# A two-block sequence model in one launch: counting the ties of the 32nd score, and loading the expert stage's weights one stage earlier

## The chip, the cores and the metric

The kernel runs on one core of a Trainium2 chip. Its time is the device time of one execution in microseconds (us); of several executions the median is given. The engines are named as in the profile: PE (TensorE matmul; PEld is its weight load), DVE (VectorE), ACT (ScalarE), POOL (GpSimd) and SP (SyncE, which here only issues transfers). All arrays are float32 unless said otherwise.

## What is computed

Four sequences of 256 tokens and 256 channels, with a context of 4096 tokens and 192 channels each, go through six residual stages in turn:

```
x = x + cross_attention(layernorm(x), ctx, ...)          # 16 heads over 4096 context tokens
x = x + linear_attention(layernorm(x), ...)              # second order, decaying, 16 heads
x = x + experts(layernorm(x), ...)                       # 8 experts, top 1, low-rank parts
x = x + topk_cross_attention(layernorm(x), ctx, ...)     # below; then a state space layer and an FFN
x = x + causal_attention(layernorm(x), ...)
x = x + fp4_linear(layernorm(x), ...)
```

The change touches the third and the fourth. The fourth keeps, for each query row and each of 4 heads, the 32 largest of the 4096 scores:

```
scores = einsum('bthd,bghd->bhtg', Q, K) / sqrt(32)
scores = where(vision_mask, scores, -inf)
topv, topi = top_k(scores, 32)
probs = softmax(topv)
attn = zeros_like(scores).at[..., topi].set(probs)
c_t = einsum('btg,bgd->btd', attn.mean(heads), V)
```

## The kernel before, in words

Everything is one program with a hand-written order for each engine. It is built of stages (`stage_x0`, `stage_hla`, `stage_moe`, `stage_x1a`, `stage_x1b`, `stage_a1`); each returns one function per engine, and each engine runs them one after the other. Between two stages stands a barrier (`stage_end`): each of the four compute engines signals its end, and every engine, SP too, waits for all the others.

**The linear attention** (`stage_hla`, about 880 to 1092 us of the span) takes its weights from `OV`, which were loaded during the first stage; its function for SP is empty (`pass`).

**The expert stage** (`stage_moe`, about 1092 to 1251 us) weaves four jobs: the experts of the 4 sequences, the convolution kernel of the later state space layer ("s4d"), and the keys of the first sequence for the next stage ("keys"). SP starts it with three loads (L1404 to L1406): `x1a` (256 KB, the projections for keys and queries), `moe` (2756 KB) and `s4d` (645.5 KB), and then the context blocks `CT` of `key_projection`, two buffers of 96 KB that are refilled as PE uses them (L1067). DVE starts with the layernorm of sequences 0 and 1 (`XN`, L204), then does the s4d setup (L1292 on), which needs `z_dt`, an exponential by ACT (L1212) from the `s4d` pack. PE starts with the first two pieces of the keys, then transposes `XN`, does two more pieces and then the gate products (`LG`).

**The selection stage** (`stage_x1a`, about 1251 to 1834 us) goes through 16 pieces p (4 sequences by 2 blocks of 128 query rows by 2 pairs of heads), two heads h in each. In outline:

- PE computes the scores of a piece in 8 parts; ACT copies them into `SC[p % 2]`, after the selection of piece p - 2 has freed it.
- DVE takes the 8 largest of each group of 128 scores (`candidates`, L1674), 32 groups, so 256 candidates in `CA` (128x256). `top(p, h)` (L1676 to L1690) then finds the 32nd value: four rounds of `match_replace` (which removes the 8 values found) and `max` (the next 8). The fourth round is there for the 33rd value alone.
- A flag per row says where the short way can't be trusted: when the 33rd value equals the 32nd, or when a group of 128 may hold more than 8 of the 32 (its 8th candidate is at least the 32nd value). PE adds up the flags of all rows (`flag`), and `check(p)` reads the sum into a register; if it isn't 0, a slow way over all 4096 scores is taken.
- ACT computes the exponentials of the piece into `PM` (`weigh`, L1604). DVE then keeps those at or above the 32nd value and sums them (`select`, L1716, a `scalar_tensor_tensor` over 4096 with its sum written out).
- POOL divides by the sums and adds the four heads up in `ACC` (L1787 to L1797): for even p a scaling (head 0), and a scaling and an addition (head 1); for odd p a scaling and an addition for both.

DVE's order in this stage: in step n it does the candidates and `top` of piece n - 1, and `check` and `select` of piece n - 2, behind the first head's candidates where n is even and in their middle where n is odd. Where n % 4 is 3 it also converts a mask row (`MR`, L1667), and where n % 4 is 1 it normalises the next queries (`XN`, L1660), both ahead of the candidates.

```
for r8 in range(4):
    if r8 > 0:
        e.wait_ge(*V.now())
    e.match_replace(CA[:, :], t8[:, 8 * r8:8 * r8 + 8], CA[:, :], SENT).then_inc(*V.up())
    e.wait_ge(*V.now())
    e.max(t8[:, 8 * r8 + 8:8 * r8 + 16], CA[:, :]).then_inc(*V.up())
```

## Time and profile before

| | |
|---|---|
| median of 3 runs | 2200.42 us (2195.33 to 2202.61) |
| the profiled execution | 2203.82 us, of which its span 2202.0 us |
| busy over the span | PE 82%, DVE 56%, ACT 47%, POOL 35% |
| DVE, 8 largest of 128 scores (L1674) | 1024 times, 275 to 277 ns |
| DVE, `top`: match_replace and max over 256 | 128 of each, 409 and 428 ns |
| DVE, `select` (L1716) | 32 times, 4484 ns |
| POOL, addition into `ACC` (L1797) | 22 times, 8872 ns |
| POOL, scalings (L1795, L1792) | 30 times, 3.68 us |
| POOL, reciprocal of a sum (L1787) | 30 times, 0.55 to 4.73 us |

The times of the profile are those of one execution. "Idle before" is how long the engine stood before an instruction, with what ended that wait. An engine that isn't the bottleneck may idle at no cost, so the busy shares over the whole span say little here: each stage has its own limit.

### The profile page before, as it was taken

To read this page: it belongs to the slowest core of one execution; us is meant where nothing else is said; L and a number is where in the kernel's file an instruction comes from. 1 tells how busy PE (TensorE), PEld (TensorE's weight loads), DVE (VectorE), ACT (ScalarE), POOL (GpSimd) and SP (SyncE) were. 2 spreads that over 40 slices of the span, in tenths; PEclk is the share of its full clock that TensorE was granted. 3 is DMA by queue.
4 is the path that set the end of the run, shared out by engine and by line. 5 is a ranking of instruction groups with operands and counts; after the bars stand their busy time and mean duration, and the time that the engine had idled before them with its cause. 6 is when DMAs were issued, how large, how long until landed. Compare 5 with 4: busy or idle time off the path is not lost. (4 is left out here: it accounts for less than half of the span.)

```text
span 2202.0 us, 34851 instructions
## 1 busy us (share of the span) xinstructions
PE 1807.5 (82%) x13676; PEld 1104.1 (50%) x13676; DVE 1233.7 (56%) x3075; ACT 1025.5 (47%) x1381; POOL 759.8 (35%) x669
## 2 busy tenths in 40 slices
PE   5969999999999898888687877877766849888874
PEld 2434554454445444556466723544444437676653
DVE  5142424333332300364578379899999995557675
ACT  1457657756765687112131145555546521214442
POOL 6343324433542230000030027777878850110000
PEclk8989999999999999999967855878787669999897
DMA  6647555655756170000120001223132252000000
GB/s 143 118 105 127 117 109 109 117 119 113 122 109 128 56 125 38 1 2 1 58 70 1 14 1 44 79 59 87 51 86 66 58 184 86 1 1 1 1 6 15
DMA packets 78046, 150.01 MB, mean 68 GB/s; under 512 B 15464, under 2 KB 63144, under 8 KB 71464
## 3 DMA queue, kind: packets, MB, share of 16 engines
q1 hardware_dynamic: 64304, 101.80, 16.5%
q0 software_dynamic: 12768, 42.59, 12.7%
q8 instruction: 118, 1.93, 0.4%
q10 hardware_dynamic: 792, 3.17, 0.4%
q14 instruction: 64, 0.52, 0.1%
HBM read 93.59 MB, written 2.62 MB: 44 GB/s over the span
## 5 line engine op out<-in xcount | busy, mean ns | idle before, releaser
L571 ACT ACTIVATE P<-R 128x1024 f32<-128x1024 f32 x512 | 506.8, 1026 | 222.3 <-PE R L112 186.3
L112 PE MATMUL R<-QS,KST 100*128 100x256 bf16 x2048 | 297.0, 277 | 60.2 <-ACT P L571 53.5
L112 PEld LDWEIGHTS R<-QS,KST 100*128 100x128 bf16 x2048 | 170.0, 98 | 224.8 <-ACT P L571 120.9
L1797 POOL TENSOR_TENSOR ACC<-ACC,PM 128x4096 f32<-128x4096 f32 x22 | 195.2, 8872 | 1.8
L200 POOL TENSOR_TENSOR LNrs<-LNve,pk_const 128x2 f32<-128x2 f32 x36 | 25.3, 703 | 462.7 <-DVE LNve L196 462.5
L112 PE MATMUL R<-OV,QT 32*128 32x512 f32 x512 | 183.0, 802 | 0.0
L789 POOL DMA_DIRECT2D KST<-OV x300 | 144.5, 490 | 71.7 <-PE R L112 55.2
L112 PE MATMUL R<-P,VP 128*32 128x256 f32 x2304 | 156.1, 388 | 5.3 <-issue 5.0
L601 DVE CAST OV<-RT 128x512 bf16<-128x512 f32 x64 | 27.7, 432 | 217.2 <-ACT RT L116 130.0
L733 POOL CAST OV<-RT 128x512 bf16<-128x512 f32 x64 | 42.6, 665 | 266.5 <-DVE RT L604 266.5
L1787 POOL TENSOR_TENSOR SM<-SM,NG 128x1 f32<-128x1 f32 x30 | 79.3, 2644 | 147.5 <-DVE PM L1716 147.5
L112 PE MATMUL B<-P,VP 128*32 128x256 f32 x1792 | 121.2, 388 | 0.0
L1674 DVE MAX8 CA<-S 128x8 f32<-128x128 f32 x512 | 101.8, 275 | 12.0 <-ACT S L116 11.6
L1674 DVE MAX8 CA<-SC 128x8 f32<-128x128 f32 x512 | 100.9, 277 | 4.8 <-ACT SC L116 4.1
L116 ACT ACTIVATE S<-R 128x1024 f32<-128x1024 f32 x64 | 64.1, 1023 | 60.1 <-DVE PM L1716 34.3
L112 PEld LDWEIGHTS R<-P,VP 128*32 128x32 f32 x2304 | 60.7, 109 | 61.9 <-issue 36.2
L112 PE MATMUL R<-OV,ONB 1*128 1x512 bf16 x256 | 62.9, 488 | 33.9 <-ACT SC L116 20.8
L112 PEld LDWEIGHTS R<-OV,QT 32*128 32x128 f32 x512 | 65.1, 251 | 38.7 <-issue 30.9
L112 PE MATMUL R<-CN,AT 128*128 128x192 f32 x288 | 67.0, 385 | 19.1 <-DMA CN<-in_ctxn 13.6
L116 ACT ACTIVATE SC<-R 128x1024 f32<-128x1024 f32 x64 | 64.1, 1020 | 39.6 <-PE R L112 24.3
L1795 POOL TENSOR_SCALAR PM<-PM,SM 128x4096 f32<-128x4096 f32 x22 | 80.9, 3679 | 2.2
L1716 DVE SCALAR_TENSOR_TENSOR PM<-SC,T,PM 128x4096 f32<-128x4096 f32 x16 | 71.1, 4484 | 9.8 <-ACT S L116 4.2
(370 smaller groups left out, 3559.0 us busy)
## 6 DMA issues: line engine op xcount, KB each, us to landing
KST<-OV POOLq DMA_DIRECT2D x276, 128.0 KB, 10.8
CT<-in_ctxP SPq DMA_DIRECT2D x40, 768.0 KB, 4.4
CN<-in_ctxn SPq DMA_DIRECT2D x60, 384.0 KB, 3.5
CT<-in_ctxT SPq DMA_DIRECT2D x64, 192.0 KB, 2.5
KST<-OV SPq DMA_DIRECT2D x84, 128.0 KB, 10.4
KST<-in_ctxP ACTq DMA_DIRECT2D x4, 768.0 KB, 9.4
QS<-x_q POOLq DMA_DIRECT2D x24, 128.0 KB, 5.4
pk_a<-in_pk_a SPq DMA_DIRECT2D x1, 3014.0 KB, 10.4
```

Of the source, the lines that this page charges most:

```text
L112: return e.matmul(o, l, r, start=st, stop=sp, skip_group_check=True)
L116: return e.activation(o, i, ACT.Copy)
L200: return e.tensor_tensor(LNrs[:, i, :], LNve[:, i, :], cst["nhalf"], ALU.pow)
L571: e.activation(P[(32 * p + k0) % 3][:, :], ring.at(("s", p, k0))[:, :], ACT.Exp).then_inc(*EX.up((p, k0)))
L601: e.tensor_copy(KS[0][:, cs], rt[:, :]).then_inc(*KD.up())
L733: e.tensor_copy(KS[1][:, cs], rt[:, :]).then_inc(*KG.up())
L789: e.dma_start(KST[buf][16 * s:16 * s + 16, hh, cols], KS[SLOT_K[s]][r0:r0 + 16, cols]).then_inc(*S[buf].up((b, g) if hh == hs[-1] and s == ...
L1674: e.max(CA[:, g * 8:g * 8 + 8], SC[p % 2][:, h, g * 128:g * 128 + 128]).then_inc(*V.up())
L1716: e.scalar_tensor_tensor(pm[:, :], SC[p % 2][:, h, :], T8[p % 2][:, h, 31:32], pm[:, :], ALU.is_ge, ALU.mult, accum_out=SM[p % 3][:, h, SU ...
L1787: e.tensor_tensor(rc, sm[:, h, SUM:SUM + 1], NG1[:, :], ALU.pow).then_inc(*G.up())
L1795: e.tensor_scalar(pm, pm, rc, 0.25, ALU.mult, ALU.mult).then_inc(*G.up())
L1797: e.tensor_tensor(acc[:, :], acc[:, :], pm, ALU.add).then_inc(*G.up(("sum", p, h)))
```

## The change

It has two parts that have nothing to do with each other.

1. **`top` and `check`.** The fourth round is dropped. In its place one `tensor_scalar` compares the 256 entries left in `CA` with the 32nd value and writes its sum out: the number of entries at or above it, which is 8 if there is no tie. The flag is then (8th candidate of a group at least the 32nd value) plus that number, so the sum over 128 rows and two heads is 2 * 128 * 8 when all is well, and `check` branches when it is anything else.

2. **The expert stage's first loads.** A new function `moe_loads` allocates the `moe` and `s4d` packs and the two `CT` buffers so that they live through both stages. SP issues the three loads and the first two `CT` blocks in the linear attention's stage, where it had nothing to do. The order among the three loads is now `s4d`, `x1a`, `moe`.

```
-        def stage_hla(c):
+        def stage_hla(c, loads):
...
             def sync(e):
-                pass
+                loads(e)
...
+        def moe_loads(c, x1a):
+            t = {nm: pack(c, nm) for nm in ("moe", "s4d")}
+            keys = key_projection(c, x1a[1])
+            LW, W4 = dsig("w_moe"), dsig("w_s4d")
+
+            def sync(e):
+                load(e, "s4d", t["s4d"][0], W4)
+                load(e, "x1a", x1a[0], LA)
+                load(e, "moe", t["moe"][0], LW)
+                keys["sync"](e, 0, 0)
...
             def sync(e):
-                load(e, "x1a", x1a[0], LA)
-                load(e, "moe", t_moe, LW)
-                load(e, "s4d", t_s4, W4)
                 for kind, *at in plan:
-                    if kind == "keys":
+                    if kind == "keys" and at[1] > 0:
                         keys["sync"](e, *at)
...
-                    for r8 in range(4):
+                    for r8 in range(3):
...
                     e.wait_ge(*V.now())
-                    e.tensor_scalar(fl, fl, t8[:, 32:33], t8[:, 31:32], ALU.max, ALU.is_ge).then_inc(*V.up(("fl", p, h)))
+                    e.tensor_scalar(CA[:, :], CA[:, :], t8[:, 31:32], 0.0, ALU.is_ge, ALU.add, accum_out=t8[:, 32:33]).then_inc(*V.up())
+                    e.wait_ge(*V.now())
+                    e.tensor_scalar(fl, fl, t8[:, 31:32], t8[:, 32:33], ALU.is_ge, ALU.add).then_inc(*V.up(("fl", p, h)))
...
-                    with e.If_ne(reg["v"], 0):
+                    with e.If_ne(reg["v"], 2 * 128 * 8):
...
-        with ExitStack() as c:
-            stages.append(stage_hla(c))
         KL = sbt(ctx, "KL", [128, 2, 256])
         x1a = pack(ctx, "x1a")
-        with ExitStack() as c:
-            stages.append(stage_moe(c, x1a))
+        with ExitStack() as both:
+            early = moe_loads(both, x1a)
+            with ExitStack() as c:
+                stages.append(stage_hla(c, early["sync"]))
+            with ExitStack() as c:
+                stages.append(stage_moe(c, early))
```

The other lines of the diff hand `bank` to `key_projection`'s functions when they are called, no longer when it is built.

On SP, around the barriers into the linear attention and out of it, the order before (OV<-in_pk_hla is the linear attention's own pack, issued in the first stage; CT_91 and CT_92 are the two context buffers):

```order
L222 DMA OV<-in_pk_hla 128x4864 [waits d_k_slots1,d_k_slots_pool1,d_k_slots_pool0,d_k_slots0]
L222 DMA pk_x1a<-in_pk_x1a 128x512 [waits stage_end_tensor,stage_end_vector,stage_end_gpsimd,stage_end_scalar]
L222 DMA pk_moe<-in_pk_moe 128x5512
L222 DMA pk_s4d<-in_pk_s4d 128x1291
L1067 DMA CT_91<-in_ctxT 96x2x256
L1067 DMA CT_92<-in_ctxT 96x2x256
L1067 DMA CT_91<-in_ctxT 96x2x256 [waits x1_key_product]
```

and in the changed kernel:

```order
L222 DMA OV<-in_pk_hla 128x4864 [waits d_k_slots1,d_k_slots_pool1,d_k_slots_pool0,d_k_slots0]
L222 DMA pk_s4d<-in_pk_s4d 128x1291 [waits stage_end_scalar,stage_end_gpsimd,stage_end_vector,stage_end_tensor]
L222 DMA pk_x1a<-in_pk_x1a 128x512
L222 DMA pk_moe<-in_pk_moe 128x5512
L1082 DMA CT_52<-in_ctxT 96x2x256
L1082 DMA CT_53<-in_ctxT 96x2x256
L1082 DMA CT_52<-in_ctxT 96x2x256 [waits stage_end_gpsimd,stage_end_scalar,x1_key_product,stage_end_vector,stage_end_tensor]
```

Before, the barrier at the end of the linear attention stood ahead of all five transfers; now it stands behind them, ahead of the third `CT` block, and they wait only for the barrier at the end of the first stage.

On DVE, one call of `top` in the selection stage before (CA holds the candidates, T the values found, SM the flag and the negated maximum):

```order
L1679 TENSOR_REDUCE SM_146<-CA 128x1
L1680 MAX T_144<-CA 128x8
L1682 TENSOR_SCALAR SM_146<-T_144 128x1
L1686 MATCH_REPLACE CA<-T_144,CA 128x256
L1688 MAX T_144<-CA 128x8
L1686 MATCH_REPLACE CA<-T_144,CA 128x256
L1688 MAX T_144<-CA 128x8
L1686 MATCH_REPLACE CA<-T_144,CA 128x256
L1688 MAX T_144<-CA 128x8
L1686 MATCH_REPLACE CA<-T_144,CA 128x256
L1688 MAX T_144<-CA 128x8
L1690 TENSOR_SCALAR SM_146<-SM_146,T_144 128x1
```

and the same call in the changed kernel:

```order
L1689 TENSOR_REDUCE SM_146<-CA 128x1
L1690 MAX T_144<-CA 128x8
L1692 TENSOR_SCALAR SM_146<-T_144 128x1
L1696 MATCH_REPLACE CA<-T_144,CA 128x256
L1698 MAX T_144<-CA 128x8
L1696 MATCH_REPLACE CA<-T_144,CA 128x256
L1698 MAX T_144<-CA 128x8
L1696 MATCH_REPLACE CA<-T_144,CA 128x256
L1698 MAX T_144<-CA 128x8
L1701 TENSOR_SCALAR CA,T_144<-CA,T_144 128x256
L1703 TENSOR_SCALAR SM_146<-SM_146,T_144 128x1
```

The fourth pair is gone and one pass over the 256 candidates with two outputs (L1701) stands in its place, so DVE has one instruction fewer in each of the 32 calls.

## Rows read from the trace of the kernel before

**Rows 1.** Busy time by stretch: start of the experts, its first 40 us, selection
```profile
core 0: us, PE busy (x) PEld busy (x) DVE busy (x) ACT busy (x) POOL busy (x), PEclk, DMA share, GB/s
1092.00:1105.00 13.00, 0.06 (x1) 0.09 (x1) 4.20 (x16) 0.42 (x1) 1.95 (x4) 0.63 0.83 318
1105.00:1145.00 40.00, 33.64 (x91) 24.13 (x92) 31.62 (x49) 15.85 (x24) 8.79 (x6) 0.54 0.23 70
...
1310.00:1834.00 524.00, 384.52 (x1696) 241.48 (x1697) 474.26 (x1500) 271.73 (x242) 383.35 (x82) 0.74 0.26 77
```

**Rows 2.** Timeline (start, duration, instruction, idle before), start of the expert stage
```profile
1092.50 0.33 SPq L222 DMA_DIRECT2D pk_x1a<-in_pk_x1a  x1
...
1097.21 0.73 DVE L204 TENSOR_SCALAR XN<-X,LNmv,LNrs 128x256 f32<-128x256 f32 x2 [0.81 <-POOL LNrs L200]
...
1104.23 0.42 ACT L1212 ACTIVATE z_dt<-pk_s4d 128x256 f32<-128x256 f32 x1 [16.57 <-DMA pk_s4d<-in_pk_s4d]
1104.75 0.42 DVE L1292 TENSOR_TENSOR z_pi<-z_dt,pk_s4d 128x256 f32<-128x256 f32 x1 [6.81 <-ACT z_dt L1212]
1104.94 3.75 PE L112 MATMUL B<-CT,pk_x1a 96*128 96x256 f32 x8 [13.45 <-DMA CT<-in_ctxT]
```

**Rows 3.** Timeline, expert stage, from the gate to the first expert product
```profile
1120.34 0.57 ACT L116 ACTIVATE OV<-B 128x512 f32<-128x512 f32 x1
...
1122.26 3.47 PE L112 MATMUL B<-pk_moe,XT 128*128 128x40 f32 x16
...
1124.13 0.24 DVE L1338 TENSOR_TENSOR LG<-B,pk_moe 128x80 f32<-128x80 f32 x1 [4.88 <-PE B L112]
...
1136.19 1.10 PE L178 MATMUL B<-pk_const,LM 128*32 128x128 f32 x4 [2.40 <-ACT OV L116]
...
1145.53 1.55 PE L112 MATMUL R<-XT,pk_moe 128*128 128x256 f32 x4
```

**Rows 4.** Timeline, DVE, the fourth round of one `top`
```profile
1486.65 0.09 DVE L1686 MATCH_VALUE_LOAD CA<-T,CA 128x8 f32 x1
...
1487.17 0.43 DVE L1688 MAX8 T<-CA 128x8 f32<-128x256 f32 x1
1487.63 0.27 DVE L1690 TENSOR_SCALAR SM<-SM,T 128x1 f32<-128x1 f32 x1
```

**Rows 5.** Prices near the added pass: durations of L1660 (min/median/max), a sum written out
```profile
L1660 DVE TENSOR_SCALAR XN<-X,MV,RSD x8: 401/410/1673, 1253.2 to 1532.9; 128x256 f32<-128x256 f32 x8
...
1578.77 0.08 DVE L1716 DVE_READ_ACCUMULATOR PM<-S,T,PM 128x1 f32 x1
```

**Rows 6.** Timeline, DVE and POOL: instructions of DVE held by POOL
```profile
1105.43 2.11 DVE L1294 TENSOR_TENSOR z_t<-pk_s4d 128x256 f32<-128x256 f32 x1
...
1523.90 8.91 POOL L1797 TENSOR_TENSOR ACC<-ACC,PM 128x4096 f32<-128x4096 f32 x1
...
1531.29 1.67 DVE L1660 TENSOR_SCALAR XN<-X,MV,RSD 128x256 f32<-128x256 f32 x1
```

**Rows 7.** Timeline, POOL's last addition of an odd piece and DVE's next `select`
```profile
1565.72 8.84 POOL L1797 TENSOR_TENSOR ACC<-ACC,PM 128x4096 f32<-128x4096 f32 x1
...
1574.36 4.48 DVE L1716 SCALAR_TENSOR_TENSOR PM<-S,T,PM 128x4096 f32<-128x4096 f32 x1 [0.60 <-DVE FI L1697]
...
1704.73 4.48 DVE L1716 SCALAR_TENSOR_TENSOR PM<-S,T,PM 128x4096 f32<-128x4096 f32 x1 [0.90 <-DVE FI L1697]
```

**Rows 8.** DVE groups (busy, mean ns, idle before and who ended it); a mask row's conversion
```profile
L1674 DVE MAX8 CA<-SC 128x8 f32<-128x128 f32 x512 | 100.9, 277 | 4.8 <-ACT SC L116 4.1
...
L1716 DVE SCALAR_TENSOR_TENSOR PM<-SC,T,PM 128x4096 f32<-128x4096 f32 x16 | 71.1, 4484 | 9.8 <-ACT S L116 4.2 <-DVE FI L1697 3.3 <-ACT PM L1604 2.4
...
1329.58 1.51 DVE L1667 TENSOR_SCALAR MR<-MU 32x128 bf16<-32x128 uint8 x1
```

**Rows 9.** Timeline, two places where the next step follows DVE
```profile
1733.59 4.49 DVE L1716 SCALAR_TENSOR_TENSOR PM<-SC,T,PM 128x4096 f32<-128x4096 f32 x1 [0.59 <-DVE FI L1697]
...
1793.79 0.24 PE L112 MATMUL B<-ON,SM 128*1 128x1 f32 x4 [8.20 <-DVE SM L1690]
```

More of the change, by code:

```diff
@@ L1051, in sync, with key_projection @@
             def sync(e):
-                pass
+                loads(e)
             return dict(tensor=tensor, vector=vector, scalar=scalar, gpsimd=gpsimd, sync=sync, slots=(ring, bank))
-        def key_projection(c, w, bank):
+        def moe_loads(c, x1a):
[7 more added lines that the diff above has]
+                keys["sync"](e, 0, 0)
+            return dict(t, keys=keys, LW=LW, W4=W4, sync=sync)
+        def key_projection(c, w):
             K1 = OV[:, 0:NK]
@@ L1067, in sync, with tensor @@
                     e.dma_start(CT[n % 2][:, :, :], src).then_inc(*CT1[n % 2].up(n))
-            def tensor(e, b, ch):
+            def tensor(e, bank, b, ch):
                 ps, free = bank.take(("k", b, ch), (KC1, (b, ch)))
@@ L1077, in tensor, with scalar @@
                     mm(e, o, w["Wk"][0:96, 1, :], CT[n % 2][:, 1, :], False, True).then_inc(*KM1.up(n))
-            def scalar(e, b, ch):
+            def scalar(e, bank, b, ch):
                 e.wait_ge(*KM1.at(16 * b + 2 * ch + 1))
@@ L1083, in key_projection, with stage_moe @@
             return dict(tensor=tensor, scalar=scalar, sync=sync)
-        def stage_moe(c, x1a):
-            t_moe, w = pack(c, "moe")
+        def stage_moe(c, early):
+            w, ws, keys, LW, W4 = early["moe"][1], early["s4d"][1], early["keys"], early["LW"], early["W4"]
             XN = [sbt(c, f"XN{i}", [128, 2, 256]) for i in range(2)]
@@ L1094, in stage_moe @@
             ring, bank = Slots(R), Slots(B2)
-            keys = key_projection(c, x1a[1], bank)
-            t_s4, ws = pack(c, "s4d")
             zs = ["dt", "pr", "pi", "den", "nden", "nr", "t0", "t1", "cr", "ci", "dr", "di", "b0"]
@@ L1105, in stage_moe @@
             z = {k: v[:, :] for k, v in Z.items()}
-            M, V, S, NP, GZ, LW = sig("moe_product"), sig("moe_vector"), sig("moe_inter"), sig("moe_root"), sig("moe_zero"), dsig("w_moe")
-            W4, V4, S4, G4, M4 = dsig("w_s4d"), sig("s4d_vector"), sig("s4d_function"), sig("s4d_outer"), sig("s4d_kernel")
+            M, V, S, NP, GZ = sig("moe_product"), sig("moe_vector"), sig("moe_inter"), sig("moe_root"), sig("moe_zero")
+            V4, S4, G4, M4 = sig("s4d_vector"), sig("s4d_function"), sig("s4d_outer"), sig("s4d_kernel")
             s4_steps = 15
@@ L1142, in tensor @@
                             e.wait_ge(*LA.at("x1a"))
-                        keys["tensor"](e, *at)
+                        keys["tensor"](e, bank, *at)
                     elif kind == "s4d" and at[0] == "kernel":
@@ L1208, in scalar @@
                     if kind == "keys":
-                        keys["scalar"](e, *at)
+                        keys["scalar"](e, bank, *at)
                     elif kind == "s4d" and at[0] == "setup":
@@ L1419, in stage_x1a @@
             ring, bank = Slots(R[0:2]), Slots([B2[0], B2[1], R[2][:, 0:512], R[2][:, 512:1024]])
-            keys = key_projection(c, w, bank)
+            keys = key_projection(c, w)
             K1, MRT = OV[:, 0:NK], OV[:, NK:NK + NK // 2].bitcast(BF16)
@@ L1576, in tensor @@
                         if n % 4 == 0 and rekeyed(n, ch):
-                            keys["tensor"](e, *rekeyed(n, ch))
+                            keys["tensor"](e, bank, *rekeyed(n, ch))
                         if n < NP:
@@ L1580, in tensor @@
                         if n % 4 == 3 and rekeyed(n, ch):
-                            keys["tensor"](e, *rekeyed(n, ch))
+                            keys["tensor"](e, bank, *rekeyed(n, ch))
                         if m is not None and n % 2 == 0 and ch in (1, 3, 5, 7):
@@ L1642, in scalar @@
                         if n % 4 == 0 and rekeyed(n, ch):
-                            keys["scalar"](e, *rekeyed(n, ch))
+                            keys["scalar"](e, bank, *rekeyed(n, ch))
                         if n < NP:
@@ L1646, in scalar @@
                         if n % 4 == 3 and rekeyed(n, ch):
-                            keys["scalar"](e, *rekeyed(n, ch))
+                            keys["scalar"](e, bank, *rekeyed(n, ch))
                         if m is not None and n % 2 == 0 and ch in (3, 5):
```

## The prediction, made before the changed kernel was run

> **What bounds the kernel now.** The table of the page gives PE 82% and DVE 56% of the span, which is an average over stages with different limits, so I read the two stages that the change touches. The view by stretches comes first [rows 1]: in the 13 us at the start of the expert stage PE is busy 0.06 us and DVE 4.2 us while the DMA engines are at 83%, so the stage opens on its loads. In the selection stage DVE is busy 474 of 524 us and POOL 383, PE 385; DVE looks like the limit. Then I read the timeline for who waits for whom.
>
> At the start of the expert stage SP issues the loads at 1092.50. DVE's second layernorm ends at 1097.94, and DVE then stands 6.81 us for ACT's `z_dt`, which waits for the `s4d` pack until 1104.23; PE has its first context block only at 1104.94, after 13.45 us [rows 2].
>
> In the selection stage the reader is to see that DVE shares its pace with POOL. A DVE instruction can be held until POOL's running one has ended: `z_t`, which has the form of `z_pi` (0.42 us, rows 2), took 2.11 us while POOL worked, and `XN`, at best 0.40 us, took 1.67: from 1531.29 to 1532.96, where POOL's addition, started at 1523.90, ended at 1532.81 [rows 2, 5, 6]. Its own 0.40 us subtracted, it was free to run at 1532.56, some 0.2 us before POOL's recorded end. And the `select` that follows an odd piece begins at 1574.36, where POOL's last addition of that piece ends at 1574.56 [rows 7]: with the same 0.2 us, just as POOL lets go. It took its normal 4.48 us, so it wasn't held, but nothing is left between the two.
>
> **Part 1, `top`.** Removed in each of 32 calls: one round, from 1486.65 to 1487.63, so 0.98 us [rows 4]. Added: one pass over 256 elements with a scalar from memory, its sum written out, and a wait. The trace has no such instruction. From below: `XN`, a `tensor_scalar` of the same size, 0.41 us when free [rows 5]. From above, if nothing holds it: `max` over 256, which starts 0.46 us before its successor [rows 4], and a read-out of the sum as behind `select`, 0.08 us [rows 5], with two gaps of about 0.04: 0.62. I take 0.58, near the upper end, because `select` with its sum runs at 4484 ns for 4096, as slow per element as anything on DVE [rows 8]. So 0.98 - 0.58 = 0.40 us a call (0.36 to 0.57), 0.8 us a piece, 12.8 us for all. The flag (L1690) keeps its form and costs the same.
>
> How much arrives? The 32 calls lie in 16 stretches of two, each ended by a `select` (the last by the flag):
> - The first stretch ends in a wait for ACT's copies, which follow PE: most of the 4.1 us [rows 8]. Nothing arrives.
> - Seven stretches follow an odd piece. POOL needs as long as DVE there [rows 7]: a `select` that comes 0.8 us earlier is held for what it came early. Four of the seven have no room. Two have a gap of 0.90 instead of 0.60 ahead of `select`, as the second one of [rows 7], so 0.3 us more room each: 0.6 us. The seventh waits for an ACT copy as well (the rest of the 4.1): nothing.
> - Three stretches end in waits for PE or ACT: the 4.2 and 2.4 us at L1716 [rows 8] (and a wait for the flag just ahead of one). They count from the `select` before, since ACT's copies wait for that one. Nothing.
> - Three have the mask row's conversion: 1.51 us for 128 elements [rows 8], held by POOL's addition as `XN` was. DVE comes 0.8 us earlier and is held 0.8 us longer. Nothing.
> - The stretch that ends at 1733.59, with only the fixed gap of 0.59, and the last, where PE has waited 8.20 us for the flag at 1793.79 and all that follows hangs on it [rows 9], give 0.8 us each: 1.6 us.
>
> Sum of part 1: 0.6 + 1.6 = 2.2 us of 12.8. With 0.57 us a call it is 2.9, with 0.36 it is 2.0. This term takes DVE's passes as unheld.
>
> A rule of the Trainium skill bears on this. By "SBUF — State Buffer", section "Who interferes with whom", DVE and GpSimd share one pair of SBUF ports as an exclusive lock: copies, casts and `tensor_scalar` can take it, two-input instructions contend with GpSimd's reads, and whoever comes second waits for the whole instruction. The trace agrees with the numbers above. The same section excepts the `tensor_scalar` that also writes out its accumulator, which is the added pass; no row here shows one. By the rule the sum is 2.2 us, and without the exception it is the slow rival below.
>
> **Part 2, the loads.** SP is empty in the linear attention, some 200 us long, and no one there waits for a transfer, so I cost the earlier transfers at nothing: 3.66 MB at the 318 GB/s of rows 1 is 12 us of transfer. If they weren't covered, that is what they would cost. The issues go past nothing but the barrier.
>
> At the new start ACT has `z_dt` long before 1097.94, so DVE goes on at once: 6.8 us earlier. PE starts its keys at about 1092.6, 12.3 us earlier. Next is the gate: DVE stood 4.88 us for it at 1124.13 [rows 3]. PE can't use its whole lead, since the gate's product needs a PSUM bank that ACT empties (`OV` at 1120.34), and that copy stands behind two sines that need DVE. They come 6.8 us earlier: the copy at 1113.6, ended by 1114.2. A gate product takes 1.75 us (16 matmuls in 3.47, two sequences), so `LG` starts at 1116.0 and not 1124.13: 8.1 us. From here all hangs on DVE and ACT: PE's transposes of `LM` at 1136.19 wait for ACT, the last two key pieces follow, and the expert products start at 1145.53 [rows 3]; I move all of this, and the rest of the stage, by 8.0 us.
>
> Bounds: if PE loses what it won elsewhere, 5 us. If PE keeps its fast clock (it had 0.54 of it in 1105 to 1145, behind the idle 13 us [rows 1], so mostly 1.2 GHz), the gate is 0.9 us shorter, and the two key pieces between 1136 and 1145.5 lose up to 3.3 us: 12.2.
>
> **Sum.** 8.0 + 2.2 = 10.2 us. The profiled execution took 2203.8, so 2193.6 by its own time; it stands 3.4 us above the median of the runs, from which I predict 2190.2.
>
> **The rivals.**
>
> *A, as worked out:* 2190.2, own range 2186 to 2195.
>
> *B, POOL doesn't hold `select`, or lets go earlier than I read:* the seven stretches after odd pieces then give up to 0.8 us each but the one tied to ACT, so 4.8 instead of 0.6, and the sum is 14.4: 2186.0. For it: no `select` in the trace is clearly held. Against it: `z_t` has two inputs as `select` has, and was held.
>
> *C, the expert products start on the slow clock:* they run at a mean of 0.88 in the trace of before, warm from 1146 on. If the new rhythm puts the rise later by 6 to 7 us of such work, the doubled time gives back about 6.5 of the 8: 2196.7. Nothing in the rows speaks for a later rise; PE's work there is the same.
>
> *D, the added pass is held by POOL (the other side):* it has the form of `XN`, and if it takes what `XN` takes, each one waits for POOL's running instruction. In a stretch after an odd piece POOL runs twice a small step (0.6), a scaling (3.68) and an addition (8.87, all in the table), so it adds from about 4.3 to 13.2 and from 17.5 to 26.4 us after the `select`. The first added pass comes at about 7 (3.2 for 16 groups, 3.9 into `top`) and waits 6 us, the second then comes at 24.4 and waits 2; 8 us by 7 is 56. After even pieces it costs about 1 us by 4, the others have room: 60 us in all, so 2200.4 - 8 + 60 = 2252. The point from which it decides: a hold of more than 0.4 us a pass eats part 1. For it: rows 5 and 6. Against it: `top`'s small `tensor_scalar` (L1690) is never held (0.27 us [rows 4], and so in all 32), so the form alone doesn't decide.
>
> *E, the count isn't 2048 and `check` branches each time:* 18 passes over 4096 a piece at about 4.4 us are 79 us, 16 pieces 1270 us: some 3460. Only if the sum is formed otherwise than the code says.
>
> **How the numbers follow.** A 0.62, B 0.14, C 0.13, D 0.08, E 0.03. The likeliest time is A's, 2190.2. From 2183 (B with half of the clock's gain) to 2198 (C and the spread of the runs) lie about 0.8 of it; D and E stay out with 0.11. 0.3% is 6.6 us, about what a measurement of this kernel can tell. Faster by more than that, below 2193.8: A but for 0.05, and B, and 0.02 of C: 0.73. Within it: the 0.05 and C: 0.16. Slower: D and E: 0.11.
>
> **What would show it.** Part 2: the `s4d`, `x1a` and `moe` loads at about 880 us; DVE's `z_pi` right behind `XN`; `LG` about 24 us after the barrier and not 32; the barrier behind the expert stage 8 us earlier. Part 1: one accumulating pass of 0.4 to 0.5 us with a read-out, 32 times; DVE's idle time not grown much, but `select` after odd pieces recorded at about 5.2 us instead of 4.48 and the mask rows' conversion at 2.3 instead of 1.5; the selection stage only 2 us shorter. It is wrong if `select` stays at 4.48 and starts right behind POOL with the stage over 5 us shorter (B), if the added pass shows microseconds (D), or if DVE has `max` over 4096 (E).

## The result, and the profile after

The changed kernel takes **2182.1 us** (median of 4 runs, 2180.4 to 2185.5) against 2197.9 for the kernel before (4 runs, 2195.0 to 2202.6): a ratio of 0.9921, 95% interval 0.9902 to 0.9941. The medians are 15.8 us apart, where 10.2 were predicted. (The ratio on record isn't the quotient of the two medians, 0.9928; by it the gain is 17.4 us, between 13.0 and 21.5.) The time itself lies 8.1 us below the predicted 2190.2 and 0.9 us below 2183, the lower end of the stated range; 2.5 of the 8.1 us are the base, since the median of 3 runs that the prediction started from became 2.5 us lower with the fourth.

The profiled execution of the changed kernel took 2185.5 us, its span 2183.7. Its time is taken apart at five instructions of DVE. Timeline of the changed kernel (start, duration, instruction, idle before), the first instruction of the linear attention, of the expert stage and of the selection stage, the last `select`, and the first layernorm behind the selection stage:

```profile
887.81 0.75 DVE L191 BATCH_NORM_STATS2 LNst<-X 128x6 f32<-128x256 f32 x2 [0.32 <-issue]
...
1088.92 0.75 DVE L191 BATCH_NORM_STATS2 LNst<-X 128x6 f32<-128x256 f32 x2 [0.23 <-issue]
...
1238.86 0.75 DVE L1751 BATCH_NORM_STATS2 CA<-X 128x6 f32<-128x256 f32 x2 [0.23 <-issue]
...
1785.82 4.47 DVE L1729 SCALAR_TENSOR_TENSOR PM<-SC,T,PM 128x4096 f32<-128x4096 f32 x1
...
1823.60 0.74 DVE L191 BATCH_NORM_STATS2 LNst<-X 128x6 f32<-128x256 f32 x2
```

The same five points in the kernel before and in the experiments give this table (us; each row is one profiled execution; "tail" is from the start of the last `select` to the next stage's layernorm, "behind" from there to the end of the span).

| kernel | before the experts | experts | selection to last `select` | tail | behind |
|---|---|---|---|---|---|
| before | 1092.5 | 158.65 | 548.13 | 39.65 | 363.11 |
| changed | 1088.9 | 149.94 | 546.96 | 37.78 | 360.10 |
| e1_top | 1086.1 | 157.13 | 546.69 | 37.84 | 360.00 |
| e2_loads | 1085.9 | 149.86 | 548.40 | 37.66 | 362.41 |
| e3_layout | 1086.6 | 157.01 | 548.26 | 39.64 | 363.17 |
| e4_after | 1087.2 | 149.71 | 547.13 | 37.78 | 360.11 |
| e5_noadd | 1083.8 | 158.14 | 543.24 | 39.24 | 362.50 |
| e6_noadd_top | 1089.8 | 156.72 | 540.09 | 38.50 | 362.84 |
| e7_extra | 1085.1 | 158.14 | 555.14 | 39.66 | 363.50 |
| e8_mask | 1086.2 | 148.46 | 542.74 | 38.26 | 360.14 |
| e9_last | 1083.7 | 156.98 | 548.22 | 37.07 | 362.81 |
| e10_butlast | 1084.0 | 156.79 | 545.07 | 39.10 | 360.53 |
| e11_pad2 | 1086.4 | 149.76 | 547.13 | 39.05 | 362.08 |
| e12_pad5 | 1086.9 | 149.88 | 547.23 | 41.41 | 359.69 |
| e13_before_pad2 | 1086.4 | 156.89 | 548.32 | 38.59 | 362.98 |
| e14_before_pad5 | 1086.9 | 156.94 | 548.12 | 39.66 | 363.10 |
| e15_s4d | 1086.4 | 155.00 | 548.03 | 37.23 | 362.75 |

These are single executions, and not always typical ones: the one of before (2203.8 us) is longer than all four that give its median, those of e5, e9, e10, e14 and e15 are the shortest of their ten. A difference of a microsecond or two in one stage counts only where several rows repeat it.

The first two rows: of 18.3 us between the two profiled executions 3.5 lie ahead of the experts, where no kernel differs in what it computes (the column runs from 1083.7 to 1092.5 over all of them; the one of before is the longest), 8.7 in the experts, 1.2 in the selection up to its last `select`, 1.9 in the tail and 3.0 behind it.

**The expert stage after.** Timeline of the changed kernel, what answers to [rows 2, 3]: the loads during the linear attention, and the stage from its first key product to the first expert product.

```profile
887.61 0.33 SPq L222 DMA_DIRECT2D pk_s4d<-in_pk_s4d  x1
887.98 0.43 SPq L222 DMA_DIRECT2D pk_x1a<-in_pk_x1a  x1
888.45 0.43 SPq L222 DMA_DIRECT2D pk_moe<-in_pk_moe  x1
...
1088.79 1.99 PE L112 MATMUL B<-CT,pk_x1a 96*128 96x256 f32 x8 [0.83 <-DVEq L183]
...
1094.31 0.42 DVE L1305 TENSOR_TENSOR z_pi<-z_dt,pk_s4d 128x256 f32<-128x256 f32 x1
...
1108.70 3.63 PE L112 MATMUL B<-pk_moe,XT 128*128 128x40 f32 x16 [5.95 <-ACT OV L116]
...
1110.74 0.24 DVE L1351 TENSOR_TENSOR LG<-B,pk_moe 128x80 f32<-128x80 f32 x1 [3.75 <-PE B L112]
...
1122.80 1.09 PE L178 MATMUL B<-pk_const,LM 128*32 128x128 f32 x4 [2.28 <-ACT OV L116]
...
1132.12 1.91 PE L112 MATMUL R<-XT,pk_moe 128*128 128x256 f32 x4
```

The reader is to see that the stage no longer opens on transfers (PE's first wait for one is 1.72 us, for the third context block, at 1092.50), that `z_pi` carries no idle time where it had 6.81 us [rows 2], that the gate still waits for ACT's copy of `OV` (5.95), and that `LG` comes 21.8 us after the stage's first DVE instruction and not 31.7. The busy times of three stretches, those of [rows 1] moved to this kernel's stages, show where PE now works:

```profile
core 0: us, PE busy (x) PEld busy (x) DVE busy (x) ACT busy (x) POOL busy (x), PEclk, DMA share, GB/s
1088.40:1101.40 13.00, 9.27 (x36) 6.90 (x36) 10.84 (x25) 5.31 (x10) 6.59 (x6) 0.87 0.30 92
1101.40:1141.40 40.00, 29.99 (x96) 22.45 (x95) 32.82 (x52) 13.25 (x21) 13.11 (x13) 0.66 0.13 40
1300.00:1818.70 518.70, 382.71 (x1696) 240.66 (x1696) 469.51 (x1470) 271.15 (x242) 381.06 (x82) 0.75 0.26 78
```

PE was idle in the first 13 us and is busy for 9.3 of them, at a granted clock of 0.87; DVE works 10.8 of them instead of 4.2.

`LG` moved by 9.9 us against the stage's start, where 8.1 were said. What lies between is a hold by POOL that got shorter. Timeline of DVE in the kernel before, then in the changed one:

```profile
1107.47 2.11 DVE L1295 TENSOR_TENSOR z_t<-pk_s4d 128x256 f32<-128x256 f32 x1
1109.61 0.43 DVE L1246 TENSOR_TENSOR z_den<-z_t,z_t 128x256 f32<-128x256 f32 x1
```

```profile
1095.32 0.42 DVE L1308 TENSOR_TENSOR z_t<-pk_s4d 128x256 f32<-128x256 f32 x1
1095.77 2.00 DVE L1259 TENSOR_TENSOR z_den<-z_t,z_t 128x256 f32<-128x256 f32 x1
```

Before, both `z_t` were held (2.11 us each); now both take 0.42 and `z_den` is held instead, which saves 1.8 us ahead of the two sines and ACT's copy of `OV`.

The earlier transfers cost nothing that can be seen: the linear attention takes 201.1 to 202.6 us in the six executions that load all there, and 201.0 to 203.1 in the ten that load nothing there. (A context block is 192 KB, as the page lists it, and not 96, so the transfers are 4.04 MB and not the 3.66 of the prediction.)

**The selection stage after.** Timeline of the changed kernel, POOL and DVE: an addition, and within it the new pass and a mask row's conversion; the pass with the read-out of its sum and the flag; POOL's last addition of an odd piece and the `select` behind it; the same for the last piece:

```profile
1309.88 8.86 POOL L1810 TENSOR_TENSOR ACC<-ACC,PM 128x4096 f32<-128x4096 f32 x1
1315.68 0.48 DVE L1701 TENSOR_SCALAR_CACHE_REDUCE CA<-CA,T 128x256 f32<-128x256 f32 x1
1316.39 2.43 DVE L1677 TENSOR_SCALAR MR<-MU 32x128 bf16<-32x128 uint8 x1
...
1419.85 0.48 DVE L1701 TENSOR_SCALAR_CACHE_REDUCE CA<-CA,T 128x256 f32<-128x256 f32 x1
1420.25 0.08 DVE L1701 DVE_READ_ACCUMULATOR CA<-CA,T 128x1 f32 x1
1420.37 0.27 DVE L1703 TENSOR_SCALAR SM<-SM,T 128x1 f32<-128x1 f32 x1
...
1419.87 8.84 POOL L1810 TENSOR_TENSOR ACC<-ACC,PM 128x4096 f32<-128x4096 f32 x1
...
1427.60 5.39 DVE L1729 SCALAR_TENSOR_TENSOR PM<-S,T,PM 128x4096 f32<-128x4096 f32 x1 [0.59 <-DVE FI L1710]
...
1772.75 8.86 POOL L1810 TENSOR_TENSOR ACC<-ACC,PM 128x4096 f32<-128x4096 f32 x1
...
1780.46 5.43 DVE L1729 SCALAR_TENSOR_TENSOR PM<-SC,T,PM 128x4096 f32<-128x4096 f32 x1 [0.60 <-DVE FI L1710]
```

The pass at 1315.68 ran its 0.48 us in the middle of an addition, the conversion right behind it lasted until that addition had ended, at 1318.7. The held time stands in the duration, not in the idle time: 5.39 and 5.43 us for an instruction that takes 4.48 when free. Take 0.91 and 0.95 us off, and the two were free at 1428.51 and 1781.41; POOL's additions ended at 1428.71 and 1781.61 by the profile, 0.20 us later both times. Groups of DVE in the changed kernel (busy, mean ns, idle before), the answer to [rows 8] and the new pass:

```profile
L1729 DVE SCALAR_TENSOR_TENSOR PM<-S,T,PM 128x4096 f32<-128x4096 f32 x16 | 75.9, 4780 | 5.7 <-DVE FI L1710 5.7
L1729 DVE SCALAR_TENSOR_TENSOR PM<-SC,T,PM 128x4096 f32<-128x4096 f32 x16 | 72.1, 4541 | 10.8 <-ACT PM L1614 4.5 <-DVE FI L1710 3.6 <-ACT S L116 2.7
L1701 DVE TENSOR_SCALAR_CACHE_REDUCE CA<-CA,T 128x256 f32<-128x256 f32 x32 | 15.3, 479 | 1.1
L1677 DVE TENSOR_SCALAR MR<-MU 32x128 bf16<-32x128 uint8 x4 | 7.6, 1911 | 0.0
```

The pass takes 479 ns on average over its 32 uses, though 23 of them lie wholly within a scaling or an addition of POOL. The mask row's conversion (`MR`) grew from a mean of 1216 to 1911 ns: its three later uses take 2.43, 2.50 and 2.50 us instead of 1.51, 1.57 and 1.57. Of the 16 first `select` of a piece seven are held, six behind odd pieces and the last one.

### The profile page after: what moved, and what is told of

The parts are those of the page before. It is cut to its first block and busy times, and to the rows that moved or that the text cites. A ratio compares the mean times of both kernels' runs of the same rounds, so it can differ in the third digit from the quotient of the medians.

```text
span 2183.7 us, 34819 instructions
## 1 busy us (share of the span) xinstructions
PE 1795.8 (82%) x13676; PEld 1097.5 (50%) x13676; DVE 1228.6 (56%) x3043; ACT 1025.0 (47%) x1381; POOL 760.2 (35%) x669
## 3 DMA queue, kind: packets, MB, share of 16 engines
q1 hardware_dynamic: 64304, 101.80, 16.7%
## 5 line engine op out<-in xcount | busy, mean ns | idle before, releaser
L112 PE MATMUL R<-CN,AT 128*128 128x192 f32 x288 | 66.4, 382 | 18.5 <-DMA CN<-in_ctxn 12.2
L1729 DVE SCALAR_TENSOR_TENSOR PM<-S,T,PM 128x4096 f32<-128x4096 f32 x16 | 75.9, 4780 | 5.7 <-DVE FI L1710 5.7
## 6 DMA issues: line engine op xcount, KB each, us to landing
KST<-OV POOLq DMA_DIRECT2D x276, 128.0 KB, 10.8
KST<-OV SPq DMA_DIRECT2D x84, 128.0 KB, 10.2
```

What stands on the lines that cost most here:

```text
L112: return e.matmul(o, l, r, start=st, stop=sp, skip_group_check=True)
L1729: e.scalar_tensor_tensor(pm[:, :], SC[p % 2][:, h, :], T8[p % 2][:, h, 31:32], pm[:, :], ALU.is_ge, ALU.mult, accum_out=SM[p % 3][:, h, SU ...
```

## The experiments

All comparisons are with the kernel before, run on the same chip in turn (the chip differs between the groups of runs); medians and ratios are of whole executions, stage lengths are those of the table.

**One part at a time.** e1 is the kernel before with the new `top` and `check`, e2 the changed kernel with the old ones, e3 has the buffers where the changed kernel has them but all loads where they were:

```
e2:   for r8 in range(4): ...           # top and check as before, loads early
e3:   the same, and in the expert stage's sync:
+                load(e, "x1a", x1a[0], LA)
+                load(e, "moe", t["moe"][0], LW)
+                load(e, "s4d", t["s4d"][0], W4)
```

> The kernel before with part 1 alone (three rounds and the counting pass). Theory (POOL paces the odd half): the saved 0.46 us a call arrives in few stretches, the selection stage 2 to 3.5 us shorter, the whole 2 to 4 us below the kernel before. Rival 'POOL holds nothing': 0.46 x 32 less the few stretches that end in waits for PE or ACT, some 9 to 11 us. Rival 'the rest is the program's layout or the state of the chip': the stages that are not touched move by as much as the selection stage.

> The changed kernel with the old top and check, so part 2 alone. Theory: the expert stage 8 to 9.5 us shorter, all other stages within 1 us, the whole 8 to 10 us below the kernel before; with e1_top it adds up to the changed kernel (11 to 13 us below). Rival: the 4 to 5 us by which the changed kernel's other stages are shorter belong to this part (earlier transfers or shifted buffers); then this run is 12 to 15 us below.

> The buffers allocated as in the changed kernel (the packs and context buffers before the linear attention), but all loads issued where and in the order they were before, and the old top. Theory: the place of buffers costs nothing, within 2 us of the kernel before in every stage and in all. Rival: the shorter untouched stages come from the layout: 3 to 5 us below the kernel before, in the linear attention and the last stages.

> The changed kernel once more, beside the kernel before and the three others on one chip. Theory: 11 to 13 us below the kernel before (the touched stages' 11.75 us), and the 4 to 5 us more that the first comparison showed were the runs' spread. Rival: 15 to 17 us again, so that a part of the gain lies outside of the touched stages.

Measured against 2197.1 us of the kernel before: e1 2191.3 (ratio 0.9976, 0.9965 to 0.9988, so 5.3 us less), e2 2186.4 (0.9956, 0.9942 to 0.9970, 9.7 less), e3 2196.4 (0.9995, 0.9985 to 1.0005), e4 2181.2 (0.9929, 0.9915 to 0.9944, 15.6 less). As whole executions the parts add up: 5.3 + 9.7 = 15.0. The layout of the buffers costs nothing. Part 2 is what was expected in the whole and in the expert stage. Part 1 isn't: up to the last `select` it gives 1.4 us (548.13 to 546.69), and yet the kernel is 5.3 us faster (2.6 to 7.7 by the interval); the profiles have the rest in the tail (1.8) and behind (3.1), where e1 doesn't differ from before by one instruction. So my theory for e1 and e4 was too small, and the rival of e4 holds: a part of the gain lies outside of the touched stages. There the parts don't add up: from the last `select` to the end e1 is 4.9 us shorter than before, e2 2.7 (with the old `top`), and the changed kernel again 4.9 and not 7.6.

**Who takes the saved time in the selection stage.** In e5 POOL's addition into `ACC` covers 1 column instead of 4096, so the heads aren't added up; e6 is e5 with part 1; e7 is the kernel before with one accumulating pass more in each `top`:

```
e5, e6:
-  e.tensor_tensor(acc[:, :], acc[:, :], pm, ALU.add)
+  e.tensor_tensor(acc[:, 0:1], acc[:, 0:1], pm[:, 0:1], ALU.add)
e7, ahead of the flag:
+  e.tensor_scalar(CA[:, :], CA[:, :], t8[:, 31:32], 0.0, ALU.is_ge, ALU.add, accum_out=t8[:, 39:40])
```

> The kernel before with POOL's addition into ACC cut to 1 of 4096 columns (the heads are then not added up; the output differs). POOL's work on an odd piece falls from 26 us to some 9, so it can hold no select and pace nothing. It is the base for e6. By itself, by the theory: XN at 0.4 and MR at about 0.25 us, never held, the selection stage shorter by 1 to 10 us.

> e5 with part 1 on top. Theory (POOL's additions eat the gain of part 1): against e5 the gain is now most of 0.46 x 32 = 14.7 us, less the stretches that end in waits for PE or ACT: 8 to 12 us, against 2 to 4 with the additions. Rival (the gain was lost to PE and ACT, POOL has no part in it): 2 to 4 us as before.

> The kernel before (four rounds) with one accumulating pass over the 256 candidates more in each call of top, 0.55 to 0.6 us with its waits. Theory: odd pieces had no room left, so that time lost there counts in full while time won does not: 1.15 us a stretch in six or seven stretches after odd pieces, in the one ending at 1733.59 and in the last, nothing or half in the six that PE, ACT or the mask row pace: 8 to 11 us slower. Rival (gain and loss are alike): 0.55/0.46 of what e1 gains, 2.5 to 5 us slower. Rival (the pass can be held by POOL): over 20 us slower.

Measured against 2197.0 us: e5 2193.9 (0.9989, 0.9969 to 1.0009; its last `select` is 4.9 us earlier), e6 2187.5 (0.9962, 0.9946 to 0.9978), e7 2205.5 (1.0038, 1.0024 to 1.0052, so 8.5 us more). Without the additions no `select` and no `MR` is held (a group of DVE in e6):

```profile
L1718 DVE SCALAR_TENSOR_TENSOR PM<-S,T,PM 128x4096 f32<-128x4096 f32 x16 | 71.1, 4482 | 5.7 <-DVE FI L1699 5.7
L1667 DVE TENSOR_SCALAR MR<-MU 32x128 bf16<-32x128 uint8 x4 | 0.8, 204 | 0.0
```

e6's expectation fell; the medians of e5 and e6, 6.4 us apart, lie between it and its rival. Part 1 brings e6's last `select` 3.15 us ahead of e5's, more than the 1.4 with the additions, but far from 8 to 12. The stretches tell why. Up to the `select` of the seventh piece POOL was indeed the one who took: its second `select` starts 2.75 us earlier in e6 than in e5 (257.96 and 255.21 us into the stage), but only 0.37 earlier in e1 than in the kernel before (259.68 and 259.31). The very next `select` waits for ACT, which copies what PE has computed, 2.72 us in e6 and 1.47 in e5, and there the lead is gone (e6 is even 0.9 us behind e5); two later waits for ACT follow. The timeline of e6, those three:

```profile
1531.18 4.48 DVE L1718 SCALAR_TENSOR_TENSOR PM<-SC,T,PM 128x4096 f32<-128x4096 f32 x1 [2.72 <-ACT S L116]
...
1659.57 4.48 DVE L1718 SCALAR_TENSOR_TENSOR PM<-SC,T,PM 128x4096 f32<-128x4096 f32 x1 [2.41 <-ACT PM L1604]
...
1722.77 4.48 DVE L1718 SCALAR_TENSOR_TENSOR PM<-SC,T,PM 128x4096 f32<-128x4096 f32 x1 [1.41 <-ACT S L116]
```

So two layers take the gain: POOL in the odd half, PE with ACT at three places, and with POOL out of the way the second one does it. e7's 8.5 us (5.3 to 11.4 by the interval) are as expected. The added pass costs 0.52 us a call, 16.7 us in all, and puts the last `select` 7.0 us later, while 0.46 us a call less, 14.7 in all, brings it only 1.4 forward. A part of what e7 added came back as shorter holds: its three later `MR` take 0.48 to 0.54 us instead of 1.51 to 1.57, two `XN` 0.58 and 0.60 instead of 1.58 and 1.67, 5.2 us together; and the first 2.25 us that e7 loses are swallowed at the same wait for ACT. In whole executions loss and gain are nearer to each other, 8.5 us of 16.7 and 5.3 of 14.7, so that the asymmetry is shown for this stage alone.

**The mask row, a faster version.** e8 is the changed kernel with `mask` called just ahead of `check` in the same step:

```
-                    if n % 4 == 3 and n // 4 + 1 < NB:
-                        mask(n // 4 + 1)
...
+                                if n % 4 == 3 and n // 4 + 1 < NB:
+                                    mask(n // 4 + 1)
                                 check(n - 2)
```

> The changed kernel with the mask row's conversion moved from the start of its step to just ahead of check, in the middle of the first head's candidates, where POOL is idle. Theory: MR takes about 0.25 us there and not 1.9 on average, and its three stretches are paced by nothing else, so 4 to 6 us below the changed kernel. Rival: PE's scores or ACT's copies pace these stretches, and the gain is under 1 us.

Measured: 2176.8 us against 2197.0 (0.9905, 0.9881 to 0.9928), so 20 us below the kernel before and some 5 below the changed one (whose ratio was 0.9929 in e4, on another chip). `MR` takes 199 ns on average, all four unheld, and the last `select` starts at 542.74 and not 546.96: 4.2 us, of which 3 times 2.3 were on offer; another 1.3 are in the profile's expert stage (148.46 us), which this edit doesn't touch. It is the fastest version of this study.

```profile
L1677 DVE TENSOR_SCALAR MR<-MU 32x128 bf16<-32x128 uint8 x4 | 0.8, 199 | 0.0
```

**Where the other 5 us come from.** e9 has part 1 in the last piece alone, e10 in all the others (`new` selects between old and new `top`, and `check` its constant):

```
e9:   new = p == NP - 1
e10:  new = p < NP - 1
+     for r8 in range(3 if new else 4):
```

> The kernel before with part 1 in the last piece alone (2 of the 32 calls). What the earlier runs showed: in the kernels with part 1 the last select of the selection stage is 1.4 us earlier, but the tail of the stage is 1.8 us and all that follows another 3.0 us shorter, with another pattern of the granted clock. Theory (the clock's pattern after the last piece hangs on when the last flag frees PE): select gains under 0.2 us here, as POOL's last addition holds it, and yet the tail and the last stages are 1 to 5 us shorter. Rival (the pattern is set further back): tail and last stages as in the kernel before, the whole within 1.5 us of it.

> The kernel before with part 1 in all pieces but the last (30 calls). Theory (POOL, PE and ACT take the gain back): the last select comes 1.2 to 1.5 us earlier, since these 30 calls gave that in the full change. The clock's pattern behind: if it hangs on the last flag alone, as in the kernel before, so the whole 1 to 2 us below it; if it hangs on the place of the stage's end, as in the changed kernel, so 5 to 6 us below.

Measured against 2196.2 us: e9 2193.5 (0.9987, 0.9976 to 0.9997), e10 2192.1 (0.9976, 0.9965 to 0.9986). In e9 the last `select` isn't earlier at all (548.22; held, 5.44 us), yet the tail is 2.6 us shorter than in the profile of before; behind it lies 362.8, not 360.1. That is within the theory's 1 to 5 us, but it can't be put down to the last flag: e2 and e15, with the old `top` throughout, have tails of 37.7 and 37.2 us too. e10 has the 360.5, with the last flag as it was. So neither the last flag nor the other 30 calls alone set the pattern. e10's last `select` is also 1.6 us ahead of e1's though it saves less: at the `select` behind the seventh piece, where e1 waited 2.71 us for ACT and PE, e10 stood only the 0.91 us for the flag. The instructions up to there are the same in both; PE's granted clock is 0.63 in e1 and 0.96 in e10 between 260 and 270 us of the stage. So the size of part 1 in this stage (0.9 to 3.1 us over the kernels that have it) itself moves with PE's clock.

The last four runs on this delay the barrier behind the selection stage by writing ACT's last copy several times. The delay can be read off PE's wait at the barrier: 0.59 us without, 1.50 with two more copies, 2.86 with five, so 0.9 and 2.3 us. (The 1.27 and 3.63 in the expectations are the difference of two tails, which hold more than that.)

```
+   for _ in range(2 if m == ML else 0):          # e12, e14: 5
+       e.activation(CS[:, m, :], bank.at(("acc", m))[:, 0:192], ACT.Copy, scale=M1F[:, m:m + 1]).then_inc(*S.up())
+       e.wait_ge(*S.now())
```

> The changed kernel with ACT's last copy of the selection stage (CS) written three times instead of once, each waited for: the barrier behind the stage comes some 0.8 to 1.0 us later and nothing else is touched. Theory (the clock's pattern in the last stages shifts with the moment at which they begin and with PE's pauses): what follows the barrier changes by up to 3 us either way, by its own clock, though its instructions are the same. Rival (the last stages are 360.1 us long in any kernel with part 1): exactly the pad, 0.8 to 1.0 us, is added.

> As e11_pad2, with the copy written six times: the barrier 2.2 to 2.6 us later. Theory: the last stages at one of the lengths seen so far (360.1, 362.4 to 362.8, 363.1 to 363.5) or another near them, so the whole 2 to 6 us above the changed kernel and not in proportion to the pad. Rival: the pad alone, 2.2 to 2.6 us.

> The kernel before, with ACT's last copy of the selection stage written three times, so that the barrier behind that stage comes 1.27 us later (as e11 showed). Theory (the length of what follows hangs on the clock's pattern at the moment it begins, whatever the kernel): it leaves its 363.1 us and comes out somewhere between 359.7 and 363.5, so the whole between 2 us less and 1.6 us more than the kernel before. Rival (363.1 us belongs to the old top, 360.1 to the new): 363.1 again, the whole 1.3 us more.

> As e13_before_pad2, with the copy written six times, the barrier 3.63 us later. Theory: again a length between 359.7 and 363.5 us behind the barrier, another than in e13; the whole 0.2 to 4 us above the kernel before. Rival: 363.1 us again, the whole 3.6 us more.

Measured: on the changed kernel, against 2196.2 us, e11 2186.8 (0.9957, 0.9940 to 0.9974) and e12 2186.3 (0.9948, 0.9931 to 0.9966); on the kernel before, against 2195.8 us, e13 2196.0 (1.0004, 0.9991 to 1.0016) and e14 2198.8 (1.0021, 1.0010 to 1.0032). On the changed kernel the pad isn't what is paid. The medians are some 5 us above the changed kernel's for either pad (by the ratios 6 and 4, and the second is within the noise of the pad alone). By the profiles the stages behind grow by 2.0 us with 0.9 us of pad, from 360.1 to 362.1; with 2.3 us they shrink to 359.7, but there PE's first 16 matmuls behind the barrier, which lie in the tail, ran at the slow clock and took 5.21 us instead of 3.69. From the last `select` to the end either pad costs about 3.2 us. On the kernel before the stages behind stay at 363.0 and 363.1, as the rival had it, and the theory fell. Its tails with the pads are 38.6 and 39.7 us, no longer than the 39.65 without, so what is left of them after the pad is 2 us shorter. The whole of e13 (2.0 us less to 3.5 more) can't tell theory and rival apart; e14 is 2.9 us above by the medians, 4.6 by the ratio.

So the same instructions behind the barrier take from 359.7 to 363.5 us: 362.4 to 363.5 in the eight kernels with the old `top`, 359.7 to 362.8 in the seven with the new one. Counted from the last `select`, the eight take 400.0 to 403.2, and the four with the new one, the additions and no pad (changed, e1, e4, e8) 397.8 to 398.4. What decides between the patterns stays open.

What the largest piece of the difference consists of can be shown. Timeline of PE near the end, first the kernel before, then the changed kernel:

```profile
2168.24 1.51 PE L112 MATMUL B<-PT,VN 128*32 128x256 f32 x16 [0.78 <-ACT PT L116]
2170.33 5.50 PE L112 MATMUL B<-pk_a,YT 128*128 128x256 f32 x16 [0.58 <-ACT YT L116]
2175.67 0.60 PE L178 MATMUL B<-pk_const,q_CQ 128*128 128x128 f32 x4
```

```profile
2152.39 0.86 PE L112 MATMUL B<-PT,VN 128*32 128x256 f32 x16 [0.78 <-ACT PT L116]
2153.84 3.69 PE L112 MATMUL B<-pk_a,YT 128*128 128x256 f32 x16 [0.58 <-ACT YT L116]
2157.36 0.60 PE L178 MATMUL B<-pk_const,q_CQ 128*128 128x128 f32 x4
```

The same 32 matmuls take 7.0 us in one and 4.6 in the other, 2.4 of the 3.0 us. Busy times of the 20 us around them, the kernel before and then the changed one, give the granted clock (the figure behind POOL's), 0.74 and 0.91:

```profile
2161.00:2181.00 20.00, 13.29 (x72) 9.65 (x72) 11.66 (x28) 4.94 (x15) 1.12 (x1) 0.74 0.00 1
```

```profile
2145.70:2165.70 20.00, 10.84 (x72) 8.17 (x72) 13.54 (x34) 4.75 (x15) 1.97 (x2) 0.91 0.04 14
```

In both the clock falls behind a pause of PE; in the kernel before PE stays at 1.2 GHz through most of this group, in the changed one it is back at 2.4 GHz before it. In the tail the clock isn't the difference, it is 0.83 in the kernel before and 0.82 in the changed one. There it is a wait for a transfer of `CN`. Timeline of PE in the kernel before, and in e9:

```profile
1816.84 2.90 PE L112 MATMUL R<-CN,AT 128*128 128x192 f32 x8 [5.67 <-DMA CN<-in_ctxn]
```

```profile
1804.80 2.90 PE L112 MATMUL R<-CN,AT 128*128 128x192 f32 x8 [3.95 <-DMA CN<-in_ctxn]
```

In the changed kernel the wait is 4.02 us, which makes 1.65 of the 1.9; over all runs it was 3.8 to 7.4 us. What moves it wasn't tested.

**Which load counts.** e15 is e2 with `s4d` alone loaded early:

```
 def sync(e):
     load(e, "s4d", t["s4d"][0], W4)
-    load(e, "x1a", x1a[0], LA)
-    load(e, "moe", t["moe"][0], LW)
-    keys["sync"](e, 0, 0)
```

What is taken out here is issued at the start of the expert stage.

> e2 with only the s4d pack loaded in the linear attention; x1a, moe and the context blocks are issued at the start of the expert stage as before. Theory (the gate hangs on DVE's setup through ACT's two sines and the copy behind them): most of the gain stays, the expert stage 6 to 7.5 us shorter than before and not 8. Rival (PE's keys and their loads are what counts): 0 to 3 us.

Measured: 2197.6 us against 2195.8 (1.0011, 0.9999 to 1.0024). My theory fell. In the profiled execution (2191.2 us, the shortest of the ten) the expert stage is 2 us shorter than in the other kernels that load late (155.0; they have 156.7 to 158.7), and in the whole nothing of it is left; the interval even leans to slower, for which I have no cause. Timeline of e15, DVE at the gate:

```profile
1113.89 0.24 DVE L1352 TENSOR_TENSOR LG<-B,pk_moe 128x80 f32<-128x80 f32 x1 [9.44 <-PE B L112]
```

DVE is there as early as in e2 and then stands 9.44 us for PE, which had waited 11.83 us for its first context block. `LG` comes 27.5 us into the stage, against 21.8 with all loads early. So `s4d` alone isn't enough: PE's keys take DVE's place at once. The other half alone (`x1a`, `moe` and the context blocks early, `s4d` late) wasn't run.

## Why the prediction was right, and where it was wrong

- **Part 2, 8.0 us: right.** The expert stage takes 149.7 to 149.9 us in five of the six executions with all loads early (148.5 in e8), and 156.7 to 158.7 in the ten with all of them late, a mean of 157.3, so 7.5 us; 8.7 between the two profiles first compared. The steps held: `LG` at 21.8 us (said: 24), the gate behind ACT's copy of `OV`, the last two key pieces at the slow clock again (3.78 and 3.75 us). `LG` and the first expert product (43.2 us into the stage and not 53.1) are 9.9 us earlier; 1.2 of it are given back by the end of the stage. That the 8.0 fits so well has some luck in it: `LG` was to come 8.1 us earlier, the shorter hold of `z_t` (1.8 us) wasn't foreseen, and what it added was mostly lost again behind the gate. That `s4d` alone would not have carried the term is shown by e15.
- **Part 1, the mechanism: right.** POOL holds `select` behind odd pieces and the mask rows, each by what DVE came early: 5.39 us (said: 5.2) and 2.43 to 2.50 (said: 2.3), `XN` likewise (mean 712 to 945 ns). B and D are out. A call saves 0.46 us and not 0.40, since the pass is 0.48 and its read-out 0.08 beside the next start.
- **Part 1, its size up to the last `select`: 1.2 us where 2.2 were said.** That the last piece gives 0.8 us was wrong: PE got its flag earlier, but the `select` behind it found POOL's addition still running and was held for 0.95 us. One of the two gaps of 0.3 us was won and lost again at the wait for PE's scores behind the seventh piece. And the stretch that was to give 0.8 us at 1733.59 gave 0.6, since its gap for the flag grew from 0.59 to 0.91.
- **The step that failed** is the sum, "8.0 + 2.2 = 10.2 us": it took all that lies outside of the two touched stretches as fixed. Behind the last `select`, where no instruction was changed, the kernel is 4.9 us shorter than before: 3.0 in the stages behind, at another pattern of the granted clock, and 1.9 in the tail, most of it a shorter wait for `CN`. That is a third of the measured gain of 15.8, and without it the time would have been in the range. In the touched stretches the sum was about right, 8.7 and 1.2 us where 8.0 and 2.2 were said, but not in how it was made up. The bounds took clock effects in, a gain (12.2 us) and a loss (C), both in the expert stage alone; none had a term for the stages behind. Why the changed kernel gets the shorter pattern stays open.
- A rule of the Trainium skill was weighed ("SBUF — State Buffer", section "Who interferes with whom"): that the `tensor_scalar` which writes out its sum is excepted from the lock between DVE and GpSimd. The traces agree: the pass at 1315.68 is one of 23 that ran unheld within POOL's work, and the plain `tensor_scalar` behind it was held.

## What to carry to other kernels

Before saving work on an engine, ask stretch by stretch who ends it: 14.7 us saved on DVE gave 1.4 in its stage, since POOL held what came early and PE's scores took the rest, while 16.7 us added cost 7.0 there; moving one small conversion out of POOL's way (e8) gave more than the whole of part 1 had in this stage. Transfers that a stage opens on are worth issuing a stage earlier, and all that its first steps need together: one of them alone gave nothing. And a difference of a few us in a stage that wasn't touched can be real and repeatable (360.10 and 360.11 us in two executions of the changed kernel) and still no merit of the change: a shift of 0.9 us undid two thirds of it.

## What the hardware showed that I had not expected

- Behind the selection stage the same instructions take 359.7 to 363.5 us, by where PE's clock is granted in full, and ahead of them in the changed kernel a delay of 0.9 us costs 3.3 by the profiles, one of 2.3 costs 3.2.
- The stages ahead of the experts took from 1083.7 to 1092.5 us over 17 executions of the same work (in some of them SP also issues the early loads there).
- The hold goes both ways: POOL's reciprocal of one value per row takes 0.55 us, and 4.73 when DVE's `select` of 4.48 us has just started (at 1397.88). Timeline of the changed kernel, POOL:

```profile
1398.05 4.73 POOL L1800 TENSOR_TENSOR SM<-SM,NG 128x1 f32<-128x1 f32 x1 [12.87 <-DVE PM L1729]
...
1415.46 0.55 POOL L1800 TENSOR_TENSOR SM<-SM,NG 128x1 f32<-128x1 f32 x1
```
